# Q, K and V projected already turned for two batches at a time, with the operands of the scores stacked by DMA

## What is computed

```python
x = x + tanh(g_xattn) * attention(layernorm(x), ctx, ctx)
x = x + tanh(g_ffn) * ffn(layernorm(x))
# attention: 32 query heads of 16, 8 key/value heads (4 query heads share one)
Q = query @ Wq + bq ; K = key @ Wk + bk ; V = value @ Wv + bv
w = softmax(Q K^T / sqrt(16)) ; y = (w V) @ Wo + bo
# ffn: y = (silu(x w1^T) * (x w3^T)) w2^T, inner width 1792, weights scaled by blocks of 128
```

## Time and profile before

| | us |
|---|---|
| median of 3 runs | 391.83 |
| lowest and highest | 391.08, 392.46 |
| the profiled execution, its own time | 391.85 |
| its span, first to last instruction | 390.1 |

### The profile page before, as it was taken

The page is one execution under the profiler, slowest core; times in us unless marked ns, Lnnn a source line. Parts: engine busy times, 40 slices in busy tenths (PEclk is TensorE's granted clock), DMA queues, the critical chain, the costliest instruction groups (busy, mean ns, idle before and its releaser), DMA issues.

```text
span 390.1 us, 6293 instructions
## 1 busy us (share of the span) xinstructions
PE 377.4 (97%) x2350; PEld 307.5 (79%) x2350; DVE 271.7 (70%) x452; ACT 209.1 (54%) x367; POOL 160.5 (41%) x135
## 2 busy tenths in 40 slices
PE   7789999999998999999999999999999999999996
PEld 5578888888887677878888888888888888888885
DVE  5978998979998967898776777543954344554334
ACT  4678999998999986552332332332332332332320
POOL 6558889898999785264333443000000000000000
PEclk9999999999999999999999999999999999999999
DMA  8903104100000040295000000000200000000002
GB/s 289 342 14 86 32 2 167 46 40 6 2 6 3 3 166 2 86 416 227 0 0 0 0 0 0 0 0 2 108 0 0 0 0 0 0 0 0 0 0 108
DMA packets 6817, 20.98 MB, mean 54 GB/s; under 512 B 875, under 2 KB 1131, under 8 KB 6668
## 3 DMA queue, kind: packets, MB, share of 16 engines
q1 hardware_dynamic: 6364, 19.92, 14.0%
q10 hardware_dynamic: 432, 0.79, 0.5%
HBM read 18.28 MB, written 2.10 MB: 52 GB/s over the span
## 4 chain that ended last, share of the span: by engine, by line
PE 83%; DVE 9%; DMA 3%; SPq 2%; ACT 1%; issue 1%; POOL 0%; DVEq 0%
PE ps L1767 23%; PE ps L1769 23%; PE ps L1768 22%; PE ps L1819 3%; PE ps L1809 3%; PE ps L1774 3%; DMA gsc<-in_small 3%; DVE MX L1142 2%; PE ps L1827 2%; PE ps L1775 1%; PE ps L1828 1%; DVE x2HL L1172 1%; DVE X L1183 1%; DVE aTL L1153 1%; DMA Qst<-Mrow 1%
## 5 line engine op out<-in xcount | busy, mean ns | idle before, releaser
L1767 PE MATMUL ps<-x2HL,w13H 128*128 128x512 f32 x224 | 89.1, 398 | 0.0
L1769 PE MATMUL ps<-x2HL,w13L 128*128 128x512 f32 x224 | 88.6, 395 | 0.0
L1768 PE MATMUL ps<-x2HL,w13H 128*128 128x512 f32 x224 | 88.4, 395 | 0.0
L340 POOL TENSOR_TENSOR PL<-E,PH 128x512 f16<-128x512 f32 x64 | 74.1, 1174 | 13.2 <-ACT E L609 7.2
L351 POOL TENSOR_TENSOR wres<-wres,gsc 128x1536 f32<-128x1536 f32 x14 | 42.5, 3037 | 44.2 <-DVE hf L1196 44.2
L632 ACT ACTIVATE T<-ps 128x512 f32<-128x512 f32 x28 | 16.7, 597 | 79.0 <-PE ps L1769 79.0
L640 ACT ACTIVATE hH<-hf 128x512 fp32r<-128x512 f32 x28 | 17.7, 632 | 63.5 <-DVE hf L1196 63.5
L1769 PEld LDWEIGHTS ps<-x2HL,w13L 128*128 128x128 f32 x224 | 42.0, 187 | 10.4
L1768 PEld LDWEIGHTS ps<-x2HL,w13H 128*128 128x128 f32 x224 | 42.0, 188 | 9.8
L1189 DVE SCALAR_TENSOR_TENSOR A<-T,ps 128x512 f32<-128x512 f32 x28 | 19.2, 685 | 43.8 <-ACT T L632 43.8
L1767 PEld LDWEIGHTS ps<-x2HL,w13H 128*128 128x128 f32 x224 | 42.0, 188 | 9.5
(11 more groups left out here) (112 smaller groups left out, 712.8 us busy)
## 6 DMA issues: line engine op xcount, KB each, us to landing
wres<-in_wff SPq DMA_DIRECT2D x14, 768.0 KB, 6.7
X<-in_x SPq DMA_DIRECT2D x8, 256.0 KB, 11.1
ct<-in_ctxt SPq DMA_DIRECT2D x7, 256.0 KB, 3.2
raw<-in_wproj SPq DMA_DIRECT2D x3, 512.0 KB, 6.3
out<-X SPq DMA_DIRECT2D x6, 256.0 KB, 2.0
raw<-in_wproj SPq DMA_DIRECT2D x1, 1024.0 KB, 9.4
Qst<-Mrow SPq DMA_DIRECT2D x32, 8.0 KB
out<-X ACTq DMA_DIRECT2D x2, 256.0 KB, 2.1
```

The source lines that it names most:

```text
L340: pool.tensor_tensor(PL[:, g % NL, :], E[:, g % NE, :], PH[:, g, :], ALU.subtract).then_inc(pL_ok, 1)
L1767: pe.matmul(out_ap, aH, bH, start=start, stop=False)
L1768: pe.matmul(out_ap, aH, bL, start=False, stop=False)
L1769: return pe.matmul(out_ap, aL, bH, start=False, stop=stop)
```

## The change

Two batches are projected at a time, and the weights are the stationary operand now, so the results come out of PE already turned (heads on the partitions): one product of 256 columns for V, one for K, and four for Q (`project_q`, one for each of the four query heads that share a key head, over all eight key heads). The columns of Wq are permuted on the host for this. The biases are now per partition and are added by the copies out of PSUM: by ACT in `k_high` and `q_high`, by DVE in `k_low`, `q_low` and `v_bias`. The products for the biases, the 24 stacking transposes of a batch and the six ACT copies after them are gone. For V the turned result has its bias added and is turned back by two transposes for two batches (`turn_v`).

The copies have all heads on the partitions once. The stacked operands are put together from them by DMA within SBUF: `keys_in` (two DMAs of 32 partitions for the high part, two of 16 for the low part, per pair of heads and two batches) and `queries_in` (two DMAs for the high part and one for the low, 64 KB each, per pair of heads and batch). That makes 64 for K and 96 for Q, 160 in all. SP issues 144 of them and ACT 16. For K, the copy of each of the two heads is made with the other head's rows multiplied by zero (`side`, `bside`), and the rows for the low parts are cleared once (`clear_keys`).

The maxima of a batch come by one DMA of 16 rows, repeated for the four pairs of heads, instead of four of 4 rows; their sign is in the selecting rows. Some work changes engine: the high part of the context goes from POOL to ACT, two of V's three parts from DVE to ACT, the low part of the maxima from DVE to POOL, the low part of Wq from DVE to POOL, and three of eight second normalisations from ACT to DVE. The order of every engine is written anew. The feed-forward part beyond its first chunks is the same.

The core of the difference:

```diff
-        ctH, ctL = (context.enter_context(nc.sbuf_tensor(n, [P, 2, DM], F32R)) for n in ("ctH", "ctL"))
+        ctH, ctL = (context.enter_context(nc.sbuf_tensor(n, [P, KB, 2, P], F32R)) for n in ("ctH", "ctL"))
...
+        KTH = sa("KTH", [P, 2, TWO], F32R)
+        KTL = sa("KTL", [P, 2, TWO], F32R)
+        xTH = sa("xTH", [P, KB, 2, P], F32R)
+        xTL = sa("xTL", [P, KB, 2, P], F32R)
+        QTH = sa("QTH", [P, 2, GJ, P], F32R)
+        QTL = sa("QTL", [P, 2, GJ, P], F32R)
+        VT = sa("VT", [P, TWO])
...
+        def keys_in(eng, n, h, low):
+            done = (k_in0, k_in1, k_in2, k_in3)[h]
+            s = (NBATCH - NKST + n % NKST) * P
+            if low:
+                for gg in range(2):
+                    r, a = 64 + 16 * gg, 32 * h + 16 * gg
+                    eng.dma_start(r32(x2HL[r:r + DH, gg, h, s:s + TWO]), r32(KTL[a:a + DH, gg, :])).then_inc(done, 16)
+            else:
+                for t in range(2):
+                    eng.dma_start(r32(x2HL[32 * t:32 * t + 32, :, h, s:s + TWO]),
+                                 r32(KTH[32 * h:32 * h + 32, :, :])).then_inc(done, 16)
+        def queries_in(eng, n, h, low):
+            done = ((q_in00, q_in01), (q_in10, q_in11), (q_in20, q_in21), (q_in30, q_in31))[h][n % 2]
+            for t in ((1,) if low else (0, 2)):
+                eng.dma_start(r32(Qst[32 * t:32 * t + 32, n % 2, h, :]),
+                             r32((QTL if low else QTH)[32 * h:32 * h + 32, n % 2, :, :])
+                             .rearrange("r j q -> r (j q)")).then_inc(done, 16)
+        def max_in(eng, n):
+            eng.dma_start(r32(Qst[ROWS:ROWS + NM, n % 2, :, :]),
+                         r32(Mrow[0:NM, :]).unsqueeze(1).broadcast_to([NM, PAIRS, GJ * P])).then_inc(mrow_in, 16)
...
-            def max_in(n, h):
-                done = (mrow_in0, mrow_in1, mrow_in2, mrow_in3)[h]
-                sp.dma_start(r32(Qst[ROWS:ROWS + 4, n % 2, h, :]), r32(Mrow[4 * h:4 * h + 4, :])).then_inc(done, 16)
...
+            sp.wait_ge(kT_H, 2)
+            keys_in(sp, 0, 2, 0)
+            sp.wait_ge(kT_L, 1)
+            keys_in(sp, 0, 2, 1)
+            keys_in(sp, 0, 0, 0)
+            keys_in(sp, 0, 0, 1)
+            keys_in(sp, 0, 1, 0)
+            sp.wait_ge(qT_L, 4)
+            queries_in(sp, 0, 0, 1)
+            queries_in(sp, 0, 1, 1)
+            queries_in(sp, 1, 1, 1)
+            queries_in(sp, 0, 2, 0)
+            queries_in(sp, 0, 2, 1)
+            queries_in(sp, 1, 2, 1)
+            queries_in(sp, 1, 3, 0)
+            keys_in(sp, 0, 3, 0)
+            queries_in(sp, 1, 0, 1)
+            queries_in(sp, 1, 1, 0)
+            queries_in(sp, 1, 0, 0)
+            queries_in(sp, 1, 2, 0)
...
+            sp.wait_ge(qT_H, 8)
+            sp.wait_ge(st_ps, 2)
+            queries_in(sp, 2, 0, 0)
+            sp.wait_ge(qT_L, 8)
+            queries_in(sp, 2, 0, 1)
+            keys_in(sp, 2, 1, 0)
+            sp.wait_ge(st_ps, 4)
+            queries_in(sp, 2, 1, 1)
+            queries_in(sp, 2, 1, 0)
+            weights_in(sp, 0)
...
-            def context_high(n):
-                pool.wait_ge(ct_in[n % NCT], 16 * (n // NCT + 1))
-                pool.tensor_tensor(ctH[:, n % 2, :], ct[:, n % NCT, :], unit[:].broadcast_to([P, DM]), ALU.mult).then_inc(ctH_ok, 1)
...
-            def k_high(bank):
-                for gg in range(2):
-                    act.activation(Ktok[:, :, gg, 0:2, gg, :],
-                                   bank[:, 0:KVD].rearrange("p (a g d) -> p a g d", a=PAIRS, g=2)[:, :, gg, :]
-                                   .unsqueeze(2).broadcast_to([P, PAIRS, 2, DH]), ACT.Copy).then_inc(ktokH, 1)
-            def q_high(bank):
-                act.activation(Qtok[:, :, 0:3:2, :], bank.rearrange("p (a d) -> p a d", d=32)
-                               .unsqueeze(2).broadcast_to([P, PAIRS * GJ, 2, 32]), ACT.Copy).then_inc(qtokH, 1)
+            def x_high(n, bank):
+                act.activation(xTH[:, :, n % 2, :], bank.rearrange("p (k n) -> p k n", k=KB), ACT.Copy).then_inc(xTH_ok, 1)
+            def k_high(bank, gg):
+                act.wait_ge(sides, 2)
+                act.activation(KTH[:, gg, :], bank[:, 0:TWO], ACT.Identity, bias=bside[:, gg:gg + 1],
+                               scale=side[:, gg:gg + 1]).then_inc(kT_H, 1)
+            def q_high(bank, j):
+                act.wait_ge(bias_in, 16)
+                act.activation(QTH[:, :, j, :], bank[:, 0:TWO].rearrange("p (b q) -> p b q", b=2), ACT.Identity,
+                               bias=biasT[:, BQ + j:BQ + j + 1]).then_inc(qT_H, 1)
...
-            def k_stacked(n, h, bank):
-                act.activation(kst(n)[0:ROWS, :, h:h + 2, :], bank[0:ROWS, :].rearrange("p (h g k) -> p g h k", h=2, g=2),
-                               ACT.Copy).then_inc(kst_ok, 1)
-            def q_stacked(n, h, bank):
-                act.activation(Qst[0:ROWS, n % 2, h, :], bank[0:ROWS, :], ACT.Copy).then_inc(qst_ok, 1)
-            def max_rows(k, bank):
+            def v_first(n, bank):
+                act.activation(v_part(n, 0), v_of(bank), ACT.Copy).then_inc(v1_ok_act, 1)
+            def v_second(n, bank):
+                act.activation(v_part(n, 1), v_of(bank), ACT.Copy).then_inc(v2_ok_act, 1)
+            def context_high(n):
+                act.wait_ge(ct_in[n % NCT], 16 * (n // NCT + 1))
+                act.activation(ctH[:, :, n % 2, :], tokens(n), ACT.Copy).then_inc(ctH_ok_act, 1)
...
-            def max_high(k):
-                dve.tensor_scalar(Mtok[:, :, :, :, 0], MX[:], -1.0, None, ALU.mult).then_inc(mH_ok, 1)
-            def max_low(k):
-                dve.scalar_tensor_tensor(out=Mtok[:, :, :, :, 1], in0=MX[:], scalar=-1.0,
-                                         in1=r32(Mtok[:, :, :, :, 0]), op0=ALU.mult, op1=ALU.subtract).then_inc(mL_ok, 1)
+            def normalise2(n):
+                dve.tensor_scalar(x2n[:], X[:, n, :], rs2[:, 0:1], nb2[:, 0:1], ALU.mult, ALU.add).then_inc(x2n_ok_dve, 1)
+            def v_bias(bank):
+                dve.wait_ge(bias_in, 16)
+                dve.tensor_scalar(VT[:], bank[:, 0:TWO], biasT[:, BV:BV + 1], None, ALU.add).then_inc(vT_ok_dve, 1)
+            def context_low(n):
+                dve.tensor_tensor(ctL[:, :, n % 2, :], tokens(n), r32(ctH[:, :, n % 2, :]), ALU.subtract).then_inc(ctL_ok_dve, 1)
...
-            def project_kv(n, bank, k):
-                project(bank, 2 * KVD, ctH[:, n % 2], ctL[:, n % 2], KV0, k)
-            def add_bias(bank, width, b0):
-                return pe.matmul(bank[:, 0:width], ones[:], brow[:, b0:b0 + width], start=False, stop=True)
-            def stack_k(h, bank):
-                for i in range(4):
-                    m = turn(bank[0:ROWS, i * P:(i + 1) * P],
-                             Ktok[:, h + i // 2, i % 2, :, :, :].rearrange("p t g d -> p (t g d)"))
-                m.then_inc(kst_ps, 1)
-            def stack_q(h, bank):
-                for j in range(GJ):
-                    m = turn(bank[0:ROWS, j * P:(j + 1) * P],
-                             Qtok[:, h * GJ + j, :, :].rearrange("p t d -> p (t d)"))
-                m.then_inc(qst_ps, 1)
+            def project_kv(bank, w0, k0, k1):
+                for k in range(k0, k1):
+                    w = slice(w0 + k * KVD, w0 + (k + 1) * KVD)
+                    m = three(bank[:, 0:TWO], WpH[:, w], WpL[:, w], ctH[:, k, :, :], ctL[:, k, :, :], k == 0, k == KB - 1)
+                return m
+            def project_q(bank, j, k0, k1):
+                for k in range(k0, k1):
+                    c = Q0 + (j // 2) * KB * TWO + k * TWO + (j % 2) * P
+                    w = slice(c, c + P)
+                    m = three(bank[:, 0:TWO], WpH[:, w], WpL[:, w], xTH[:, k, :, :], xTL[:, k, :, :], k == 0, k == KB - 1)
+                return m
+            def turn_v(bank):
+                for b in range(2):
+                    m = turn(bank[:, b * P:(b + 1) * P], VT[:, b * P:(b + 1) * P])
+                return m
```

More of the change, by code:

```diff
@@ L686, in _ @@
[L686 to L697 removed]
+            act.wait_ge(q_ps, 3)
+            q_high(W0, 2)
+            gates()
+            keys_in(act, 0, 3, 1)
@@ new lines, in _ @@
+            act.wait_ge(kT_L, 2)
+            keys_in(act, 2, 3, 1)
+            act.wait_ge(q_ps, 5)
+            act.wait_ge(q_in01, 48)
+            act.wait_ge(q_in11, 48)
+            act.wait_ge(q_in21, 48)
+            act.wait_ge(q_in30, 48)
+            act.wait_ge(q_in31, 48)
+            q_high(W1, 0)
+            act.wait_ge(q_ps, 6)
+            q_high(W2, 1)
+            context_high(5)
+            act.wait_ge(mT_ps, 1)
+            max_rows(W0)
+            act.wait_ge(mrows, 1)
@@ L702, in _ @@
+            max_in(act, 0)
+            act.wait_ge(vt_ps, 2)
+            v_first(2, W2)
+            act.wait_ge(r1_ok, 2)
+            v_second(2, W2)
+            act.wait_ge(q_ps, 7)
+            q_high(W1, 2)
+            act.wait_ge(nb1_ok, 5)
+            normalise(4)
+            act.wait_ge(q_ps, 8)
```

(19 more changed lines are left out.)

2457 lines of the change are left out of this document (1200 added, 1257 removed).

## The result

The changed kernel is slower: 406.86 us median of 4 runs against 392.14 (391.08 to 392.50) beside it, a ratio of 1.036 (95% interval 1.031 to 1.041). One of the four took 905.57 us, which is not explained here; it counts in that median, while the ratio goes by the other three and a fifth run (404.78 to 408.17, median 405.7). The forecast was 384 (376 to 394). The profiled execution took 408.17 us.

What follows compares the result with a forecast made beforehand. ACT was taken as fullest in the first 152.9 us, POOL and DVE close behind. Start 39 + stage 104 + wait 1.5 = 144.5, 8.4 less, so 391.85 - 8.4 = 383.5, said as 384 us (376 to 394).

Steps and rivals of the forecast that it cites:

- Loads: Work per engine in the stage of the exponentials after the change: ACT 94 us, DVE 92, POOL 97 to 100.
- PE's relief of 18 us: In the stage, PE loses transposes, bias products and projections moved ahead of it, so it does not become the bound.
- The stage of 98 / 0.94 = 104 us: First transposed scores to last PL: POOL, then fullest, reaches the 0.94 busy share ACT had before, giving 104 us.
- So they are hidden by 0.8 us in the tightest place (batch 2) and by over 2 elsewhere.: Query DMAs in the stage take 4.1 us, and PE reaches the scores needing them 4.9 to 8 us later.
- The one wait without cover is the copy of Q ahead of PH: At the start of batch 2's exponentials, ACT's copy waits 4.1 us with 2.6 us of other work; charged 1.5.
- Rival 2: DMAs land late and hold PE's scores of batches 2 to 7 from a 4.7 us landing: 407 us, 17% chance.
- The start: Up to the first transposed scores: two batches projected first and DMAs in series move it from 33.1 to 39 us.
- The clock: PE's granted clock should stay at 1.00; if thinner work between 19 and 33 us lowers it, the start is later.
- The 1.5 us for the copy of Q: Charge in the sum for ACT's uncovered wait at the start of batch 2's exponentials: 1.5 us.
- Rival 1: Relief in the stage does not show and no engine's busy share rises: 392 us, or 389 with smaller loads; 20% chance.
- a closed ring: Cause given for no gain in the stage: PE, ACT and POOL wait for each other in a circle.
- signs of being wrong: First scores_t after 43, landing over 4.7 us for Qst<-QTH, PE waiting for queries, POOL below 90% and waiting.

Runs made afterwards that it cites:

- g1: f3 with both high copies of a pair of heads in one DMA, 112 stacking DMAs instead of 160, part of the computation left out: 387.8 us.
- k2: f3 with the low keys masked to go in one DMA instead of two, and the maxima's DMA cut in two: 395.8 us.
- h5: f3 with 8 key transfers of each of batches 4 and 6 issued by ACT instead of SP, all 160 kept: 402.9 us.
- h3: f3 with queries from batch 2 on stacked through HBM, and low keys masked to go in one DMA: 408.3 us.
- g3: f3 without renewing stacked queries from batch 2 and keys from batch 4 on, part of the computation left out: 395.4 us.
- e3: Changed kernel with superfluous products added in three of PE's waits, nothing removed: 403.2 us.
- e1: Changed kernel with the DMA of the maxima of batches 1, 3 and 5 issued by ACT instead of SP: 406.3 us.
- e2: Changed kernel with the queries of batches 0 and 1 brought by one DMA for both batches: 408.3 us.
- e4: Changed kernel with the edits of e1 and e2 together: 404.1 us.
- k1: f3 with low keys masked (one DMA) and batch 1's stacked queries as zeros instead of 12 transfers, part left out: 394.7 us.
- f3: Changed kernel with three weight loads later, maxima of batches 1, 3, 5 issued by ACT, batch 0's output-bias addition ahead of its first row maximum: 402.2 us.
- f1: Changed kernel with SP's three 768 KB weight loads in the stage issued two to eight transfers later: 404.0 us.

## Why the prediction was wrong

- **Loads: right for three engines.** ACT, DVE and POOL within 1 to 2 us, the rest behind the stage too. PE's relief of 18 us was 8.6, and 16.3 in g1, where the clock was 1.00. The stage of 98 / 0.94 = 104 us was 106.9 in g1, which leaves out part of the work, and 111.5 in k2, the best complete version.
- **The step that failed** is "So they are hidden by 0.8 us in the tightest place (batch 2) and by over 2 elsewhere." I took three issues and one landing for a group, as if SP were free when it was due. I had counted for every engine but SP: 78.0 of 123.3 us of issue, and two stretches of over 22 us without a wait. The keys, 16 DMAs for each pair of batches, and the maxima stand in the same line, so each waits for what is ahead. PE waited 3.3 us in the stage for queries, and 10.5 for the maxima, to which the sum gave nothing there: "The one wait without cover is the copy of Q ahead of PH" was wrong too. The gaps between batches grew by 15.8 us, more than the 12.4 won within them. With 48 transfers fewer the stage lost 12.3 us (119.2 to 106.9). That the number of transfers costs this is shown; whether by SP's line, by their landings or by both is not separated (h5, h3 and g3 speak against SP's issue time alone).
- **Landing times were a small part.** Rival 2 said that the DMAs come late, and its 407 is what came, but mostly by another mechanism, so the number is luck: it began at a landing of 4.7 us, and the median was 2.0 for Qst<-QTH. What was late was mostly the issue. But rival 2 also named the weight loads, and ahead of batch 1 they played the part it gave them: behind the one issued at 52.4 the `sel` landed after 6.0 us, a QTL after 4.9 and the maxima after 4.5 (medians 2.9, 2.0 and 3.3).
- **The start: the term was too small.** 39 forecast, 45.1 measured. First scores 27.3 instead of 24; the DMAs of the block were issued by 36.6 instead of 31.8, the copy of the maxima started at 40.7. Part is the doubled work, part the half clock (0.59 and 0.72 in 10 to 15 us). I named this clock and gave it no price. It stayed at 42.7 to 47.8 in every run, whatever was done to the transfers. How much each part has is not settled. So the cause of these 6.1 us stays open.
- **The clock: named, not priced.** It fell in PE's idle in the gaps. With three waits filled (e3) it was 1.00 in the stage and the time some 3 us less, not clear of noise; g1 has 1.00 by itself.
- **The 1.5 us for the copy of Q** that waits for DMAs ahead of PH was not seen as a wait of its own: ACT waited 0.5 us for Qst<-QTL in the stage.
- **Rival 1** (the relief does not show) described the shares, but its cause, a closed ring, was wrong: in g1 the same loads fit in 106.9 us.
- **Its signs.** Of the signs of being wrong that the prediction lists, these came: a first `scores_t` after 43, PE waiting for the queries, and POOL below 90% (77%), waiting for ACT. PE's waits for DMAs in the stage were 13.8 us instead of below 3.

## What to carry to other kernels

Give the engine that issues DMAs a row of its own in the sum: number of issues times the duration of one, and not only against the length of the whole stage (63% here) but for each stretch between two points where something is due. Where it issues without a pause, a transfer waits for all ahead of it, and its landing time alone does not tell when it arrives. Where a change replaces computing by many small transfers, count the transfers first. What helped here was fewer on the way from producer to consumer; another queue and a detour with larger ones did not.

## What the runs showed of the hardware

An operation of DVE waited for one of POOL though no semaphore joins them. Timeline of the changed kernel, DVE and POOL, and then of e1:

```profile
29.17 0.68 DVE L1294 TENSOR_TENSOR X<-X,boT 128x512 f32<-128x512 f32 x1
...
29.21 5.04 POOL L477 TENSOR_TENSOR WpL<-raw,WpH 128x2048 fp32r<-128x2048 f32 x1 [1.69 <-ACT WpH L721]
```

```profile
29.98 4.87 DVE L1297 TENSOR_TENSOR X<-X,boT 128x512 f32<-128x512 f32 x1
...
29.79 4.50 POOL L474 TENSOR_TENSOR WpL<-raw,WpH 128x2048 fp32r<-128x2048 f32 x1 [1.74 <-ACT WpH L718]
```

Begun 0.04 us ahead of POOL's, the addition took 0.68 us, and POOL's took 5.04 instead of 4.50. Begun behind it, it took 4.87 (e1), 4.09 (e2) and 3.37 us (e4), and ended 0.55 us behind POOL's each time. The Trainium skill (SBUF — State Buffer, "SBUF: two separate sides") says that DVE with two SBUF inputs and a GpSimd operation that reads SBUF hold a shared port pair as an exclusive lock; the traces agree, in both directions.

The granted clock was 0.50 in the windows behind PE's gaps of some 4 us in the changed kernel, and which gaps it fell in differed between the versions. It also differs between executions of one kernel, and the time with it: k1 took 391.6 us in the one with a mean clock of 1.00, 393.2 to 395.7 in those with 0.983 to 0.996, and 396.1 to 397.8 in those with 0.977 and 0.978. Which of the two is the cause is not shown. Times of such versions vary more than those of the kernel before (f3 401.2 to 404.1, the kernel before 390.9 to 392.3 beside it).

Small transfers landed late beside a 768 KB load, and not only on the queue of the load: in e1 the `sel` on SP's queue took 7.4 us and the maxima on ACT's 7.5, at medians of 2.8 and 3.4. With the load moved (f1) the longest landing of `sel` was 2.9. An issue of a stacking transfer held SP for a median of 0.59 us, at 16 KB (KTL) as at 64 KB (QTH).
